# Narrow passes of a graph network: 17 columns on TensorE, eleven gathers, and two of five one-hot blocks made on ScalarE

## The reference

```python
# layer 0
m = tanh(x[src] * edge_weight[:, None]);  h = segment_sum(m, dst)
# layer 1: attention over edges (16 x 16 weights an edge), softmax per destination, per component
# layer 2
h = segment_max(x[src] * edge_weight1, dst) @ W.T + b
# layer 3: twice
agg = segment_sum(x[src], dst);  h = relu(((1 + eps) * x + agg) @ wa + ba) @ wb + bb
# after each layer: x = layernorm(x + h)
```

## Time and profile before

| | |
|---|---|
| median of 3 runs | 8105.31 us (8102.64 to 8106.66) |
| span of the profiled execution | 8106.3 us, 1.0 above the median; no other time of it is given |
| busy: PE, DVE, POOL, ACT | 7107.4, 6896.2, 5221.6, 2239.6 us |
| matmuls of the narrow passes (L823) | 60,480 |
| TensorE in the passes, from | 89.7, 4599.1, 5760.8 and 6931.6 us |

### The profile page before, as it was taken

How to read it: one execution, slowest core, us unless ns; L and a number is a source line. 1 busy time by engine, 2 the same in 40 slices (tenths; PEclk the granted TensorE clock), 3 DMA queues, 4 the chain that set the end, 5 groups by cost and what they waited for, 6 DMA issues and landing times.

```text
span 8106.3 us, 209725 instructions
## 1 busy us (share of the span) xinstructions
PE 7107.4 (88%) x77871; PEld 6661.2 (82%) x77871; DVE 6896.2 (85%) x12224; ACT 2239.6 (28%) x7389; POOL 5221.6 (64%) x4570
## 2 busy tenths in 40 slices
PE   5999985999999999999995399998599996899994
PEld 5999984777777787777774399998599996899994
DVE  7999985999999999999997688888588885788884
ACT  0000003666666666666664100000000000000000
POOL 3555557888888888888886555555555555455554
PEclk9999997999999999999997699999799998899997
DMA  2223222555555555555554211111111111111110
GB/s 84 85 87 88 84 56 81 159 158 159 159 160 160 160 160 160 159 158 158 159 160 134 65 49 46 48 49 40 36 49 45 49 49 28 43 49 49 49 45 22
DMA packets 738222, 757.28 MB, mean 93 GB/s; under 512 B 153760, under 2 KB 698336, under 8 KB 738112
## 3 DMA queue, kind: packets, MB, share of 16 engines
q1 hardware_dynamic: 592640, 667.34, 24.9%
q0 software_dynamic: 140528, 86.77, 7.1%
q10 hardware_dynamic: 5008, 2.59, 0.1%
HBM read 239.80 MB, written 519.73 MB: 94 GB/s over the span
## 4 chain that ended last, share of the span: by engine, by line
PE 42%; DVE 29%; issue 23%; POOL 4%; DMA 1%; DVEq 1%; ACT 0%; ACTq 0%; another core or an unknown queue 0%; POOLq 0%; SPq 0%
PE ps L823 42%; DVE amax_room L1232 7%; DVE spare L1237 4%; DVE flat L1259 3%; DVE flat L954 2%; POOL got L456 2%; DVE msg L1137 2%; DVE stt L954 2%; DVE spare L1241 1%; DVE run L1158 1%; DVE wide_buf L954 1%; DVE raw L954 1%; POOL wide_buf L456 1%; DVE junk L1164 1%; DVE wide_buf L1116 1%
## 5 line engine op out<-in xcount | busy, mean ns | idle before, releaser
L456 POOL DMA_INDIRECT msg<-feat,cidx x1680 | 1681.5, 1001 | 1594.4 <-PE ps L823 1109.8
L823 PE MATMUL ps<-parts,wide_buf 128*128 128x160 bf16 x30240 | 2128.9, 233 | 289.0 <-DVE wide_buf L1116 276.4
L823 PEld LDWEIGHTS ps<-parts,wide_buf 128*128 128x128 bf16 x30240 | 2102.5, 98 | 304.8 <-issue 288.2
L456 POOL DMA_INDIRECT hsrc<-feat,aidx x1568 | 1921.5, 1225 | 461.1 <-issue 445.5
L823 PE MATMUL ps<-parts,flat 128*128 128x160 bf16 x30240 | 2118.5, 233 | 29.7 <-DVE flat L1116 16.7
L823 PEld LDWEIGHTS ps<-parts,flat 128*128 128x128 bf16 x30240 | 2093.3, 98 | 43.1 <-DVE flat L1116 21.4
L870 PEld LDWEIGHTS ps<-wsb,zT 102*128 102x128 f32 x9408 | 1462.9, 190 | 217.8 <-ACT zT L690 196.3
L870 PE MATMUL ps<-wsb,zT 102*128 102x192 f32 (+1 forms) x9408 | 1539.8, 313 | 99.0 <-ACT zT L690 98.5
L954 DVE TENSOR_TENSOR raw<-ps,amask 128x960 f32<-128x960 f32 x448 | 738.4, 1657 | 468.1 <-PE ps L823 286.5
L1137 DVE TENSOR_REDUCE msg<-raw 128x288 f32<-128x2880 f32 x224 | 1129.9, 5044 | 7.7
L657 ACT ACTIVATE cidx<-sidx 128x10 int32 (+1 forms) x224 | 46.8, 211 | 3684.6 <-DMA msg<-feat,cidx 3065.6
(11 more groups left out here) (220 smaller groups left out, 5229.9 us busy)
## 6 DMA issues: line engine op xcount, KB each, us to landing
state_tab<-flat SPq DMA_DIRECT2D x784, 512.0 KB
raw<-quot_tab SPq DMA_DIRECT2D x224, 576.0 KB
run_tab<-run SPq DMA_DIRECT2D x224, 224.0 KB
top_tab<-spare SPq DMA_DIRECT2D x392, 128.0 KB
msg<-feat,cidx POOLq DMA_INDIRECT x1680
hsrc<-feat,aidx POOLq DMA_INDIRECT x1568
efs<-in_ef SPq DMA_DIRECT2D x392, 34.0 KB
msg<-in_x,cidx POOLq DMA_INDIRECT x560
```

Source lines behind the costliest of these rows:

```text
L456: return pool.indirect_dma_start(dest, None, table, rows_at(idx))
L823: last = nc.tensor.matmul(block.rearrange("p (q c) -> p q c", c=D), hot[s][:, m, t * P:(t + 1) * P], parts[:, m * Q:(m + 1) * Q, part, :], ...
```

## The change

Constants: R goes from 18 to 17, so A = U - R from 10 to 11 gathers a group. The PSUM block of a column is laid out with the ten candidates of a feature side by side (`(c q)` for `(q c)`), and so are `parts` and `picked`. VectorE makes blocks 0 to 2 (HM = 3); ScalarE makes blocks 3 and 4, each with two activations, Abs(m' - quot) into a scratch tile `apart` and Relu(1 - that) into `hot`. A new semaphore `rest` tells that they are there; TensorE and SP wait for it as well as for `hot`. ScalarE's order in a group: the first block of the next group, the tanh of the group before (pass 0), the index copy, the second block. In passes 0 and 1 it waits at the opening for `s_enter`, which VectorE raises where it sets `run` to zero. `narrow_open` makes both blocks of group 1. The masked product is in three pieces: own banks (6 columns), the last bank (2 columns, `s_rest`), the other shared banks (9 columns). `split` goes by way of a rearranged copy in `junk`.

```diff
-R = 18
+R = 17
+HM = MB - 2
+BANKS = OWN // CB
+LAST = (R - OWN) % CB
+WIDE = 4 * DC * DD
-        parts = sb("parts", [P, MB * Q, 3, D], BF)
+        parts = sb("parts", [P, MB, 3, D, Q], BF)
+        apart = sb("apart", [P, R * P], BF)
-        wide_buf = sb("wide_buf", [P, 7 * R * P // 2])
+        wide_buf = sb("wide_buf", [P, WIDE])
-        flat = sb("flat", [P, 7 * R * P // 2])
+        flat = sb("flat", [P, WIDE])
-        picked = raw[...].rearrange("p (r q c) -> p r q c", q=Q, c=D)
+        picked = raw[...].rearrange("p (r c q) -> p r c q", q=Q, c=D)
...
                             sp.wait_ge(q["hot"][1 - s], done + j + 1 + s)
+                            sp.wait_ge(q["rest"][1 - s], done + j + 1 + s)
...
-            pool.memset(parts[:, NB:MB * Q], 0.0).then_inc(s_zero, 1)
...
+            def differences(n, j, s, first, ready=True):
+                act.wait_ge(q["quot"][s], 16 * (n * HALF + j + 1))
+                if not first:
+                    act.wait_ge(q["pick"][s], (n * HALF + j) * A)
+                if ready:
+                    act.wait_ge(q["rest"][1 - s], n * HALF + j + s)
+
+            def block(s, m):
+                if parted[0]:
+                    act.wait_ge(s_apart, parted[0])
+                nc.scalar.activation(apart[:], quot[:, s, :], ACT.Abs, bias=count[:, m:m + 1], scale=-1.0).then_inc(s_apart, 1)
+                parted[0] += 1
+                act.wait_ge(s_apart, parted[0])
+                ins = nc.scalar.activation(hot[s][:, m, :], apart[:], ACT.Relu, bias=1.0, scale=-1.0)
+                if m < MB - 1:
+                    parted[0] += 1
+                    return ins.then_inc(s_apart, 1)
+                return ins.then_inc(q["rest"][s], 1)
+
+            def narrow_group(n, j, s, more):
+                b, jb = 1 - s, j - 1 + s
+                if more:
+                    differences(n, j + s, b, False)
+                    for m in range(HM, MB - 1):
+                        block(b, m)
+                if n == 0:
+                    act.wait_ge(q["mul"][b], jb + 1)
+                    nc.scalar.activation(val[:, b], val[:, b], ACT.Tanh).then_inc(q["act"][b], 1)
+                if more:
+                    act.wait_ge(q["got"][b], (n * HALF + jb + 1) * (16 * A))
+                    next_indices(2 * j + s + 1, b)
+                if more:
+                    block(b, MB - 1)
+
+            def narrow_pass(n):
+                for s in range(2):
+                    next_indices(s, s)
+                apart_start()
+                if n < 2:
+                    act.wait_ge(s_enter, n + 1)
+                differences(n, 0, 0, n == 0, n > 0)
+                for m in range(HM, MB):
+                    block(0, m)
+                apart_start()
+                narrow_open(n)
+                narrow_group(n, 0, 1, True)
+                with act.Fori(1, HALF - 1) as j:
+                    apart_start()
+                    for s in range(2):
+                        narrow_group(n, j, s, True)
...
                     pe.wait_ge(q["hot"][s], done + j + 1)
+                    pe.wait_ge(q["rest"][s], done + j + 1)
...
+                            pe.wait_ge(s_rest, n * NG + 2 * j + s)
                             pe.wait_ge(s_share, n * NG + 2 * j + s)
...
-                                    block.rearrange("p (q c) -> p q c", c=D),
-                                    hot[s][:, m, t * P:(t + 1) * P], parts[:, m * Q:(m + 1) * Q, part, :],
+                                    block.rearrange("p (c q) -> p c q", q=Q),
+                                    hot[s][:, m, t * P:(t + 1) * P], parts[:, m, part],
...
+                left = junk[:, 0:MB * QW].rearrange("p (m c q) -> p m c q", c=D, q=Q)
+                whole = NB // Q
+                link(v.memset(left[:, whole], 0.0))
+                link(v.tensor_copy(left[:, 0:whole], features[:, 0:whole * Q].rearrange("p (m q) c -> p m c q", q=Q)))
+                link(v.tensor_copy(left[:, whole, :, 0:NB - whole * Q], features[:, whole * Q:NB].rearrange("p q c -> p c q")))
...
-                    for m in range(MB):
+                    for m in range(HM):
...
+                    tt(picked[:, 0:OWN], mine_banks[s], mask_rows(0, OWN), ALU.mult).then_inc(q["read"][s], 1)
                     dve.wait_ge(q["pick"][s], (done + j + 1) * A)
+                    tt(picked[:, R - LAST:R], shared[:, (R - OWN) // CB, 0:LAST * QW], mask_rows(R - LAST, R), ALU.mult).then_inc(s_rest, 1)
+                    tt(picked[:, OWN:R - LAST], shared[:, 0:(R - OWN) // CB], mask_rows(OWN, R - LAST), ALU.mult).then_inc(s_share, 1)
...
-                    hold(v.tensor_reduce(msg[:, s, A:U, :], picked.rearrange("p r q c -> p r c q"), AX.X, ALU.add))
+                    hold(v.tensor_reduce(msg[:, s, A:U, :], picked, AX.X, ALU.add))
...
-                link(v.memset(run[:, 1, U - 1, :], 0.0))
+                v.memset(run[:, 1, U - 1, :], 0.0).then_inc(s_enter, 1)
+                dve.wait_ge(s_enter, n + 1)
```

More of the change, by code:

```diff
@@ L58 @@
 OI = 14
+HM = MB - 2
+BANKS = OWN // CB
+LAST = (R - OWN) % CB
+WIDE = 4 * DC * DD
+assert MB * R * P // 2 <= WIDE and 4 * K <= WIDE and NS * P <= WIDE
 assert NB % 2 == 1 and SL < NG // 2 and NB % DC == 0 and K % (2 * G) == 0 and NG % 2 == 0 and 2 * G == 8
 CONT, BOTH, CONT_NEG, BOTH_NEG = range(4)
-assert MB * (Q - 1) < NB <= MB * Q and CB * QW <= 512 and OWN == 2 * CB and R - OWN == 4 * CB and K % DW == 0
+assert MB * (Q - 1) < NB <= MB * Q and CB * QW <= 512 and OWN % CB == 0 and 2 * OWN // CB + -(-(R - OWN) // CB) <= 8 and K % DW == 0
 FP = mybir.dt.float32
@@ L224, in gnn_program @@
         msgs = [ps[:, s * G:(s + 1) * G, DD:2 * DD] for s in range(2)]
-        mine_banks = [ps[:, 2 * s:2 * s + 2, 0:CB * QW] for s in range(2)]
-        shared = ps[:, 4:8, 0:CB * QW]
+        mine_banks = [ps[:, BANKS * s:BANKS * (s + 1), 0:CB * QW] for s in range(2)]
+        shared = ps[:, 2 * BANKS:8, 0:CB * QW]
         s_list = sem("s_list")
@@ L285, in gnn_program @@
         s_share = sem("s_share")
-        NARROW = ("idx", "quot", "hot", "pick", "read", "got", "mul", "act", "run", "put")
+        s_enter = sem("s_enter")
+        s_apart = sem("s_apart")
+        s_count = sem("s_count")
+        s_rest = sem("s_rest")
+        NARROW = ("idx", "quot", "hot", "rest", "pick", "read", "got", "mul", "act", "run", "put")
         narrow = {k: ring(f"n_{k}") for k in NARROW}
@@ L342, in narrow_pass @@
                 sp.wait_ge(q["hot"][0], done + 1)
+                sp.wait_ge(q["rest"][0], done + 1)
                 load_quot(2, 0)
@@ new lines, in _, with apart_start @@
+            parted = [0]
+            def apart_start():
+                parted[0] = 0
+                act.sem_clear(s_apart)
+            def narrow_group(n, j, s, more):
[12 more added lines that the diff above has]
+                    block(b, MB - 1)
@@ L665, in index_pass, with narrow_open @@
+            def narrow_open(n):
+                differences(n, 0, 1, n == 0)
+                for m in range(HM, MB):
+                    block(1, m)
+            def narrow_pass(n):
                 for s in range(2):
                     next_indices(s, s)
[L667 to L676, removed]
@@ L678, in _ @@
-            act.wait_ge(s_sidx, 16)
[L679 to L683, removed]
+                apart_start()
+                if n < 2:
+                    act.wait_ge(s_enter, n + 1)
+                differences(n, 0, 0, n == 0, n > 0)
+                for m in range(HM, MB):
+                    block(0, m)
+                apart_start()
+                narrow_open(n)
@@ new lines, in narrow_pass @@
+                narrow_group(n, 0, 1, True)
[3 more added lines that the diff above has]
+                        narrow_group(n, j, s, True)
+                apart_start()
+                narrow_group(n, HALF - 1, 0, True)
+                narrow_group(n, HALF - 1, 1, False)
+                if n == 0:
+                    act.wait_ge(q["mul"][1], HALF)
+                    nc.scalar.activation(val[:, 1], val[:, 1], ACT.Tanh).then_inc(q["act"][1], 1)
@@ L684, in _ @@
+            act.wait_ge(s_sidx, 16)
+            act.wait_ge(s_count, 1)
+            narrow_pass(0)
             asked(st3[:], st2[:], ACT.Sqrt)
@@ L767, in _ @@
             asked(st3[:], st2[:], ACT.Sqrt)
-            index_pass(1)
+            narrow_pass(1)
             dense(0)
@@ L771, in _ @@
             for n in (2, 3):
-                index_pass(n)
+                narrow_pass(n)
                 dense(2 * n - 3)
@@ L964, in split @@
             def split(features):
-                link(v.tensor_copy(parts[:, 0:NB, 0, :], features[:]))
-                link(tt(nt[:], features[:], parts[:, 0:NB, 0, :], ALU.subtract))
-                link(v.tensor_copy(parts[:, 0:NB, 1, :], nt[:]))
-                link(tt(nt[:], nt[:], parts[:, 0:NB, 1, :], ALU.subtract))
-                v.tensor_copy(parts[:, 0:NB, 2, :], nt[:]).then_inc(s_parts, 1)
```

(10 more changed lines are left out.)

13 lines of the change are left out of this document (4 added, 9 removed).

## The result

The changed kernel takes 8232.85 us (median of 4 runs, 8231.87 to 8239.14) against 8105.16 for the kernel before (4 runs). The ratio is 1.0157, 95% interval 1.0145 to 1.017: 1.6% slower where 3.5% faster was forecast. The profiled execution's span is 8231.9 us.

A forecast was written before the change was run, and what follows sets the result against it. TensorE's matmuls were taken to bound passes 1 to 3 and VectorE pass 0. Savings of 174 + 117 + 8 less 18 at openings gave 281 us: 7826 us forecast, 7800 to 7880 to hold 8 in 10.

The forecast's parts named there:

- What bounds the kernel: TensorE's matmul count sets passes 1 to 3, 18.67 us a lap with no gap; VectorE sets pass 0, 19.75 us.
- Seventeen columns: TensorE: 15 matmuls of 69.15 ns leave each group, lap 17.63 us; 174 us saved in passes 1 to 3.
- 174 + 117: Savings in us inside the passes: 174 in passes 1 to 3, 117 in pass 0, all running at 17.63 us laps.
- VectorE's round: Pass 0: fewer one-hots (-1.6) and a contiguous reduction (-2.05) cut VectorE's 19.64 us to 16.0, under TensorE's 17.63.
- ScalarE's blocks: Four activations of 2,176 elements a group, 2.0 to 2.1 us each, hidden with 5.9 us to spare in pass 0.
- The eleventh gather: POOL: eleven gathers and pass 0's slice gather take 15.6 of 17.63 us a lap; claimed cost nothing.
- Openings: Start of each pass: TensorE begins later by 6.7, 4.9, 3.4 and 3.4 us; +18 in sum (13 to 22).
- the closing: End of each pass: the shorter reduction after the last matmul saves 2.0 us, 8 over four passes.
- The sum: Whole kernel: 174 + 117 + 8 - 18 = 281 us saved; span 7825, runs' median forecast 7826.
- POOL's gathers slip: Rival in pass 0: slow gather issues make laps 0.5 to 1 us longer, 7855 to 7880 us; chance 0.05.
- ScalarE sets the lap: Slower rival: a group's second ScalarE block reaches TensorE late; 8470 us if an activation takes 5 us; chance 0.03.
- The signs named for "wrong": Lap over 17.7 with TensorE waiting for Relu or one-hots, matmul spacing other than 69 ns, or reduction near 4.8 us.

The follow-up runs named there:

- even pacing: Changed kernel, with the first gather of a group also waiting until TensorE has finished the group before; 8101.2 us.
- the wide matmul, paced: Changed kernel, pacing waits kept, one matmul of 480 columns in place of three of 160, output left out; 7749.3 us.
- the one without pacing: Changed kernel without POOL's waits on TensorE's progress between the gathers of a group; 10386.7 us.

## Why the prediction was wrong, step by step

**What bounds the kernel.** Right as far as it went. But "no gap" was read from one lap. Over 600 us of pass 2 the kernel before has 15 gaps for "issue", 6.2 us in all; in pass 0 there were 52, 21 us. They were the warning that was passed over.

**Seventeen columns.** Right in itself. With plain transfers for the gathers of the columns the four passes take 989.0 to 990.5 us each and save 313 us together; the terms of the forecast, 174 + 117, are 291, and the rest is of the size of the small gaps of the kernel before. Matmuls still follow each other at 69 ns whenever nothing holds them: contiguous operands gave nothing.

**VectorE's round.** Right. The reduction takes 2.986 us (3.0 forecast), three one-hots 2.18 in the timeline (2.1), the three products 1.158 + 0.492 + 1.647 = 3.30 (3.22). VectorE waits for TensorE in pass 0 too.

**ScalarE's blocks.** The work is right: 2.107 and 2.017 us, and hidden: in the lap shown ScalarE has both blocks ready 8.4 us after it starts, TensorE needs them at 6332.98, 16.1 us after. The wait was costed at nothing, and with eleven gathers it was not: moving it off TensorE's count brought 93 us (8232.9 to 8140.3). With ten gathers the laps of passes 1 to 3 are 18.68 with it; with even pacing it costs 6 us between two single runs, next to nothing.

**The eleventh gather: "Nothing".** This is the step that failed. It was priced on POOL alone: 15.6 us of issues fit into 17.63, and POOL is indeed on time. What was never asked is what an indexed issue does to the engine that it runs beside. The change took 15 pairs out of a lap and put one gather in; TensorE then lost 1.5 us a lap in passes 1 to 3 and 3.0 in pass 0, where the slice makes twelve. In us: the passes take 4393.7 against 3959.4 with plain transfers, 434 us lost. 313 gained less 434 is the 121 by which the passes grew.

Not all of it is the eleventh gather's. With the eleventh alone made plain the passes still lose 163 of the 434 us (a half of it in pass 0, where the slice is an eleventh indexed issue), so the eleventh gather accounts for 271. The other ten cost next to nothing in laps of 270 pairs (18.68 for 18.67) and 0.3 us in laps of 255: taking a column out made the lap shorter, and the same ten gathers lie closer in it.

That indexed gathers do it is shown (plain ones, no wait for "issue"; the eleventh plain, 278 us back). Whether it is POOL's work for them or the scattered rows that they read is not shown. That TensorE is short of instructions meanwhile is supported by the wide matmul, paced, but no run shows it directly.

Where it happens stays open. The Trainium skill, "Runtime: NRT & Kernel Launch", Instruction fetch mechanics, says that an engine's instruction memory is refilled in blocks by a DMA of its own, and that this is mostly hidden. The instruction queues carried 22 and 24 packets in the whole changed kernel and 22 and 23 in the one without pacing, which lost 2.1 ms more, so as far as the traces record them, refills by that way are not what grew. Its page "SBUF — State Buffer", Who interferes with whom, says that a DMA never contends with a compute engine. The plain transfers agree (no wait for "issue" inside the four passes); the indexed ones do not in their effect, whatever the place where they meet.

**Openings.** +18 us forecast. Pass 0 opened at 96.1 (96.3 forecast). The stretches before passes 2 and 3 grew by 4.6 and 4.4, where +3.4 at the opening less 2.0 at the closing was forecast. The stretch before pass 1 shrank by 10.7: in all kernels with 17 columns it is 3388 to 3392 us, with 18 it is 3399 to 3406. It comes from attention and not from the opening: from the first to the last gather of attention's sources it is 14 us less, and one of its products on VectorE (512 elements, 392 times) takes 684 ns for 736. Why it does with 17 columns is open.

**The sum.** 281 us off the median of 8105.31 is 7824: the 1 us between span and median was put on where it had to come off. Nothing hangs on it.

**The rivals.** None was it. "POOL's gathers slip" named the right engine and the wrong direction: POOL was not late, it made TensorE late. "ScalarE sets the lap" was the only slower one, and TensorE's waits for ScalarE in passes are nil. The signs named for "wrong" looked for a wait with a name, or another matmul spacing; the wait that came has the name "issue". Slower had a chance of 0.03 in the forecast, and almost all of that was ScalarE's.

## What to carry to other kernels

Price a transfer not only on the queue that issues it but on the engines that run meanwhile: an edit that trades matmuls for indexed gathers on GpSimd can lose more than the matmuls cost, and here one gather a lap more was enough, with TensorE on 255 short pairs a lap. Look for small "issue" gaps over a whole stage before you call an engine its bound, since they show what is nearly short. Space indexed gathers, by waits on the busy engine's progress: worth 132 us here with eleven, 17 with ten. Fewer, wider instructions on TensorE, where the sums allow them, took the loss away in passes 1 to 3, though here only in a run that leaves the output out.

## What was not expected of the hardware

- 11 indexed issues in 17.6 us hold TensorE up, 10 in 18.7 hardly do; back to back (1.25 us each) they bring it down to one to four matmuls in 0.7 to 2.1 us, and the granted clock falls to 0.50 on top. Plain transfers from the same queue, with as many packets and bytes, do nothing, even unpaced.
- TensorE's increments of a semaphore come late at such times too: in the lap shown, two engines started some 3 us after the group's last matmul; with plain transfers it is 0.04 us (6318.42 to 6318.46).
- A reduction over ten contiguous elements takes 2,986 ns for 2,720, and took 5,044 for 2,880 at a stride of 16.
